# Two graph layers on one Trainium2 core: layer 1's aggregation made of three single-pass products instead of one fp32 product

## What is computed

```python
# layer 0: four bilinear scores, one picked by the code in adj (0 or 1 here)
e_k = leaky((h * a_k) @ h.T)                      # slope 0.2
alpha = sigmoid(where(adj == k + 1, e_k, -inf))
x = layernorm(x + alpha @ h + bias)
# layer 1
H = x @ W;  s = H @ a_src;  d = H @ a_dst
e = where(adj != 0, exp(-leaky(s[:, None] + d[None, :])), 0)
x = layernorm(x + elu((e @ H) / e.sum(-1)))
```

## Time and profile before

| | us |
|---|---|
| median of three runs | 1340.65 (1339.58 to 1341.52) |
| the profiled execution | 1340.03 |
| its span, first to last instruction | 1338.2 |
| one graph in the middle | 80.80 |
| TensorE busy | 1278.7 (96%) |
| VectorE, ScalarE, GpSimd busy | 1011.8, 855.6, 780.4 |
| TensorE's granted clock | 0.995 of full |

### The profile page before, as it was taken

How to read it: one execution, slowest core, us unless ns; L and a number is a source line. 1 busy time by engine, 2 the same in 40 slices (tenths; PEclk the granted TensorE clock), 3 DMA queues, 4 the chain that set the end, 5 groups by cost and what they waited for, 6 DMA issues and landing times.

```text
span 1338.2 us, 27323 instructions
## 1 busy us (share of the span) xinstructions
PE 1278.7 (96%) x7874; PEld 1142.2 (85%) x7874; DVE 1011.8 (76%) x2594; ACT 855.6 (64%) x2130; POOL 780.4 (58%) x1116
## 2 busy tenths in 40 slices
PE   5899999999999999999999999999999999999986
PEld 4888889898898988889888898988989888898875
DVE  4677778778787877778777787877878777787864
ACT  4756757576575766757577575766757567575643
POOL 3746648375573855638465583755738465483732
PEclk9999999999999999999999999999999999999999
DMA  9383480925629174380925719165380834709001
GB/s 208 64 157 92 97 145 12 186 65 118 125 39 171 49 141 110 77 159 15 173 78 106 137 27 177 55 133 114 56 183 16 161 90 98 141 18 189 25 5 34
DMA packets 223632, 135.29 MB, mean 101 GB/s; under 512 B 141168, under 2 KB 207088, under 8 KB 223600
## 3 DMA queue, kind: packets, MB, share of 16 engines
q1 hardware_dynamic: 188528, 84.57, 27.0%
q0 software_dynamic: 35072, 50.34, 23.4%
HBM read 101.32 MB, written 16.78 MB: 88 GB/s over the span
## 4 chain that ended last, share of the span: by engine, by line
PE 39%; POOL 24%; DVE 19%; issue 10%; ACT 6%; DMA 0%; DVEq 0%; POOLq 0%; ACTq 0%
POOL coef_lo L380 14%; PE acc_bank L1232 10%; PE hh_bank L1211 7%; DVE coef L885 5%; PE lg_bank L1113 4%; PE acc_bank L1115 3%; PE acc_bank L1113 3%; PE acc_bank L1114 3%; PE lg_bank L1115 3%; PE lg_bank L1114 3%; POOL rstd L401 3%; POOL rstd L391 2%; POOL var_eps L388 2%; DVE stats L925 2%; DVE reluP L920 2%
## 5 line engine op out<-in xcount | busy, mean ns | idle before, releaser
L1232 PE MATMUL acc_bank<-H,coef 128*128 128x258 f32 x2048 | 468.9, 382 | 10.9 <-ACT reluP L611 9.6
L1232 PEld LDWEIGHTS acc_bank<-H,coef 128*128 128x128 f32 x2048 | 381.6, 190 | 73.6 <-issue 20.2
L380 POOL TENSOR_TENSOR coef_lo<-coef,coef_hi 128x1024 fp32r<-128x1024 f32 x128 | 304.4, 2379 | 93.1 <-ACT coef_hi L557 93.1
L1113 PE MATMUL acc_bank<-h_hi,coef_hi 128*128 128x256 f32 x1024 | 302.7, 296 | 0.0
L1115 PE MATMUL acc_bank<-h_hi,coef_lo 128*128 128x256 f32 x1024 | 285.0, 278 | 0.0
L1114 PE MATMUL acc_bank<-h_lo,coef_hi 128*128 128x256 f32 x1024 | 284.9, 278 | 0.0
L885 DVE SCALAR_TENSOR_TENSOR coef<-tr_bank,E_col,codeT 128x256 f32<-128x256 f32 x512 | 209.2, 476 | 40.1 <-PE acc_bank L1232 36.8
L1113 PEld LDWEIGHTS acc_bank<-h_hi,coef_hi 128*128 128x128 f32 x1024 | 193.2, 189 | 3.2
L1114 PEld LDWEIGHTS acc_bank<-h_lo,coef_hi 128*128 128x128 f32 x1024 | 193.8, 189 | 1.8
L1115 PEld LDWEIGHTS acc_bank<-h_hi,coef_lo 128*128 128x128 f32 x1024 | 193.2, 189 | 0.0
L557 ACT ACTIVATE coef_hi<-coef 128x1024 fp32r<-128x1024 f32 x128 | 136.1, 1063 | 71.9 <-DVE coef L824 71.2
(11 more groups left out here) (77 smaller groups left out, 2192.3 us busy)
## 6 DMA issues: line engine op xcount, KB each, us to landing
code_nat<-in_adj POOLq DMA_DIRECT2D x128, 256.0 KB, 5.7
x_raw<-in_x SPq DMA_DIRECT2D x16, 1024.0 KB, 5.6
xb<-bias_bc SPq DMA_DIRECT2D x16, 1024.0 KB, 9.1
xb<-in_x POOLq DMA_DIRECT2D x16, 1024.0 KB, 12.3
out<-x SPq DMA_DIRECT2D x128, 128.0 KB, 1.7
codeT<-code_nat SPq DMA_TRANSPOSE x128, 3.8
W_ext<-in_L_gnn_W SPq DMA_DIRECT2D x1, 256.0 KB, 4.0
eluE<-in_L_gnn_a SPq DMA_DIRECT2D x1, 256.0 KB, 5.3
```

The lines of the kernel that those rows point to most:

```text
L380: nc.gpsimd.tensor_tensor(coef_lo[:, t % 4, :, :], blocks(coef[:, t % 4, :]), f32(coef_hi[:, t % 4, :, :]), ALU.subtract).then_inc(S.lo0, 1)
L1113: nc.tensor.matmul(dst, lhs_hi, rhs_hi, start=first, stop=False)
L1232: ins = nc.tensor.matmul(acc_bank[t % 2][:, 0:HC], coef[:, SLOT1[t], J * P:(J + 1) * P], H[:, J, :], start=J == 0, stop=J == NT - 1)
```

## The change

What it does, part by part:

- H is kept as `H_hi` and `H_lo` (fp32r), and aggregation 1 becomes three single-pass products a block on `coef_hi` and `coef_lo`, as in layer 0. The two extra `coef` buffers go; both layers share four (`t % 4`).
- ScalarE gets `high1` for each tile of layer 1, GpSimd `low1`. Tile 0 is split in two parts: blocks 0 to 4 ahead (`high1_begin`, `low1_begin`), 5 to 7 later.
- H of tiles 0 to 4 is staged in `xb` and split in one go (`high_H_first` on ScalarE, `low_H_first` on GpSimd). H of tiles 5 to 7 is written to `H_hi` directly, and VectorE makes `H_lo` (`low_H`). Projections 6 and 7 and the next graph's first wait for that.
- The masks of tiles 0 to 3 are made by instructions of four tiles (512 columns), those of 4, 5 and 6, 7 by pairs.
- `reluP` and its statistics have four buffers for two; the exponential goes to the free half of `xt_bank` in PSUM, one buffer, for two in SBUF. `power1` and the norms take two tiles at a time and come later.
- Chunk 2 moves on TensorE from behind transposes 6 to step 7, ahead of projection 5.
- SyncE also waits for `H_first_lo` before it fills `xb`; `add_x` and the low parts of x move later on GpSimd.

```diff
             def aggregate1(S, b, t):
-                pe.wait_ge(S.mask1, NT * b + t + 1)
+                pe.wait_ge(S.lo1, NT * b + t + 1)
...
                 for J in range(NT):
-                    ins = nc.tensor.matmul(acc_bank[t % 2][:, 0:HC], coef[:, SLOT1[t], J * P:(J + 1) * P],
-                                           H[:, J, :], start=J == 0, stop=J == NT - 1)
+                    ins = split_products(acc_bank[t % 2][:, 0:HC], coef_hi[:, t % 4, J, :], coef_lo[:, t % 4, J, :],
+                                         H_hi[:, J, :], H_lo[:, J, :], J == 0, J == NT - 1)
...
+            def low1(S, b, t, j0=0):
+                pool.wait_ge(S.hi1, NT * b + t + 1)
+                nc.gpsimd.tensor_tensor(coef_lo[:, t % 4, j0:NT, :], blocks(coef[:, t % 4, j0 * P:N]),
+                                        f32(coef_hi[:, t % 4, j0:NT, :]), ALU.subtract).then_inc(S.lo1, 1)
+            def low_H_first(b):
+                pool.wait_ge(F.H_first, b + 1)
+                nc.gpsimd.tensor_tensor(H_lo[:, 0:FIRST, 0:D], xb[:, 0:FIRST, :], f32(H_hi[:, 0:FIRST, 0:D]),
+                                        ALU.subtract).then_inc(F.H_first_lo, 1)
...
+                low1_begin(b)
                 if nxt:
                     low_x(F, b + 1, 0)
-                    add_x(b + 1)
...
+                low1(F, b, 0, EDGE)
+                for t in range(1, 4):
+                    low1(F, b, t)
+                for t in range(4, NT):
+                    low1(F, b, t)
+                    if nxt and t < 7:
+                        low_x(F, b + 1, t - 3)
+                    if nxt and t == 5:
+                        add_x(b + 1)
+                    if t == 5:
+                        power1(F, b, 0, 2)
+                power1(F, b, 2, 2)
+                if nxt:
+                    low0(F, b + 1, 0)
+                    low0(F, b + 1, 1)
+                power1(F, b, 4, 2)
+                if nxt:
+                    low0(F, b + 1, 2)
+                    low0(F, b + 1, 3)
...
+            def low_H(S, b, t):
+                dve.wait_ge(S.H, NT * b + t + 1)
+                nc.vector.scalar_tensor_tensor(H_lo[:, t, 0:D], hh_bank[:, 0:D], scale_col[:, t:t + 1],
+                                               f32(H_hi[:, t, 0:D]), ALU.mult, ALU.subtract).then_inc(S.H_lo, 1)
...
+                low_H(F, b, 5)
                 if nxt:
                     leaky_scores(b + 1, 3)
+                low_H(F, b, 6)
                 if nxt:
                     leaky_scores(b + 1, 4)
-                mask1_pair(b, 0, prev, EDGE, NT)
+                mask1_tiles(b, 0, 4, EDGE, NT)
+                low_H(F, b, 7)
+                ends_H_lo(F, b)
                 watch_sd(F, b, prev)
                 if nxt:
                     leaky_scores(b + 1, 5)
-                mask1_pair(b, 2, prev, EDGE, NT)
-                if nxt:
                     leaky_scores(b + 1, 6)
                 keep_watch(b, prev)
...
+                if nxt:
+                    leaky_scores(b + 1, 7)
+                mask1_tiles(b, 4, 2)
+                row_inverse(F, b, 0, prev)
+                if nxt:
+                    leaky_scores(b + 1, 8)
+                for t in range(NT):
+                    if t >= 3:
+                        row_inverse(F, b, t, prev)
+                    if t >= 4 and nxt:
+                        mask0_below(b + 1, t - 4, True)
+                        mask0_rest(b + 1, t - 4)
+                    residual1(F, b, t, prev)
+                    stats1(F, b, t)
+                    moments1(F, b, t)
                     if t < 2:
-                        mask1_pair(b, 2 * t + 4, prev)
+                        row_inverse(F, b, t + 1, prev)
+                    if t == 0:
+                        if nxt:
+                            leaky_row(b + 1, 3)
+                        mask1_tiles(b, 6, 2)
                     if nxt and t == 1:
-                        leaky_row(b + 1, 3)
...
+                        leaky_row(b + 1, 4)
```

More of the change, by code:

```diff
@@ L81, in __init__ @@
         self.H = sem(tag + "H")
+        self.H_lo = sem(tag + "H_lo")
+        if not general:
+            self.H_first = sem(tag + "H_first")
+            self.H_first_lo = sem(tag + "H_first_lo")
         self.ones = sem(tag + "ones")
-        self.squares = sem(tag + "squares")
+        self.ones_lo = sem(tag + "ones_lo")
         self.range_seen = sem(tag + "range_seen")
@@ L192, in two_graph_layers @@
         watch_max = sb("watch_max", [P, NT])
-        coef = sb("coef", [P, 6, N])
+        coef = sb("coef", [P, 4, N])
         coef_hi = sb("coef_hi", [P, 4, NT, P], FP32R)
@@ L296, in graph @@
                 if nxt:
-                    sp.wait_ge(F.resid0, NT * b + NT)
-                    sp.sem_inc(sp_past, 1)
+                    for made, count in ((F.resid0, NT * b + NT), (F.H_first_lo, b + 1)):
+                        sp.wait_ge(made, count)
+                        sp.sem_inc(past, 1)
                     fill_bias()
@@ L590, in keep_H, with high_H_first @@
                 act.wait_ge(S.scale, NT * b + t + 1)
-                nc.scalar.activation(H[:, t, 0:D], hh_bank[:, 0:D], ACT.Copy,
+                nc.scalar.activation(xb[:, t, :] if S is F and t < FIRST else H_hi[:, t, 0:D], hh_bank[:, 0:D], ACT.Copy,
                                      scale=scale_col[:, t:t + 1]).then_inc(S.H, 1)
+            def high_H_first(b):
+                act.wait_ge(F.H, NT * b + FIRST)
+                nc.scalar.activation(H_hi[:, 0:FIRST, 0:D], xb[:, 0:FIRST, :], ACT.Copy).then_inc(F.H_first, 1)
             def ends_H(S, b):
-                nc.scalar.activation(H[:, :, D], scale_col[:, :], ACT.Copy).then_inc(S.ones, 1)
+                nc.scalar.activation(H_hi[:, :, D], scale_col[:, :], ACT.Copy).then_inc(S.ones, 1)
             def last_G(b):
@@ L616, in norm1 @@
                 act.wait_ge(S.shift1, NT * b + t + 1)
-                nc.scalar.activation(x1[:, t, :], reluP[:, t % 2, :], ACT.Identity, bias=shift[:, t % 2, :],
-                                     scale=rstd[:, 2 + t % 2, :]).then_inc(S.y, 1)
+                nc.scalar.activation(x1[:, t, :], reluP[:, t % 4, :], ACT.Identity, bias=shift[:, t % 4, :],
+                                     scale=rstd[:, 2 + t % 4, :]).then_inc(S.y, 1)
             def graph(b, prev, nxt):
                 for t in range(NT + 1):
+                    if nxt and t == 8:
+                        scale_scores(b + 1, 2)
                     if t >= 3:
@@ L633, in graph @@
                     if t == 5 and prev:
+                        norm1(F, b - 1, NT - 2)
                         norm1(F, b - 1, NT - 1)
-                    if nxt and 6 <= t:
+                    if nxt and 6 <= t < 8:
                         scale_scores(b + 1, t - 6)
@@ L736, in _ @@
                         act.wait_ge(GEN.leaky1, NT * b + t + 1)
-                        nc.scalar.activation(coef[:, SLOT1[t], :], coef[:, SLOT1[t], :], ACT.Exp,
+                        nc.scalar.activation(coef[:, t % 4, :], coef[:, t % 4, :], ACT.Exp,
                                              scale=-1.0).then_inc(GEN.exp1, 1)
+                        high1(GEN, b, t)
                         elu_parts(GEN, b, t)
@@ L750, in _ @@
             dve.wait_ge(setup_step, 3)
-            nc.vector.tensor_copy(H[:, :, D + 1], sd_sq[:, :, 0]).then_inc(setup_step, 1)
+            for part in (H_hi, H_lo):
+                nc.vector.tensor_copy(part[:, :, D + 1], sd_sq[:, :, 0]).then_inc(setup_step, 1)
             def extend_weights(which, col):
                 for dt in range(KD):
-                    steps = 4 + 4 * (1 - which) + 2 * dt
+                    steps = 5 + 4 * (1 - which) + 2 * dt
                     dve.wait_ge(setup_step, steps)
```

297 lines of the change are left out of this document (168 added, 129 removed).

## The result

| | before | after |
|---|---|---|
| median, us | 1340.68 (1339.58 to 1341.52) | 1410.38 (1407.98 to 1410.77) |
| profiled span | 1338.2 | 1408.7 |
| one graph in the middle | 80.80 | 85.50 |
| mean granted TensorE clock | 0.995 | 0.973 |

The ratio is 1.0517 (95% interval 1.0498 to 1.0535): 70 us slower, where 16 us faster was forecast, and outside the range. The rows of after are read against those of before.

What follows compares the result with a forecast made beforehand. TensorE bounds the kernel, VectorE nearly as late. VectorE's 651.5 + 34.55 work + 8.7 waits gave 694.75, 1.0 us less a graph; with 1.5 in the last graph, 1340.03 - 16.5 = 1323.5, forecast 1324, range 1284 to 1352.

Steps and rivals of the forecast that it cites:

- part (b) of the waits: VectorE instructions with two SBUF inputs wait until GpSimd's instruction is over: 5.6 us a graph.
- TensorE's gain: Aggregation 1 tiles fall from 3.49 to 2.83 us: 0.66 us a tile, 84 us in 16 graphs.
- The head: Start of aggregation 1: ScalarE's new split and VectorE's difference of H 5 delay projections 6 and 7, 0.8 us lost.
- VectorE's chain: VectorE from E of tile 7 to residual 0 of the next graph: 34.55 us work plus 8.7 us waits.
- The waits for relu 0 to 3: VectorE waits for ScalarE, whose relus come after splits and scaling, before the residuals: 3.1 us a graph.
- The masks: Layer 0 masks of tiles 0 to 3 held by GpSimd differences: 1.3 us for the first, 1.8 for the others.
- The watch operations: Small VectorE operations and H's end column in aggregation 1, held by GpSimd differences: 1.2 and 1.3 us.
- My own test for rival 1: In the new trace, watch operations keeping 0.16 us and TensorE 99% busy would show TensorE stays the bound.
- rival 1: TensorE stays the bound, VectorE's waits under 4.45 us a graph: 1256, or 1284 with waits of 6 us; chance 0.23.
- rival 2: Slower: GpSimd's layer 1 differences stop VectorE, deciding from 9.7 us of waits; 1367, or 1350 at 10.4 us; chance 0.27.
- the seven meetings: Four masks, end column, range pair and code watch meeting GpSimd differences, on average 1.2 us each, 8.4 us.
- Rival 3: Three products not faster where weights are loaded three times: at or above 1340; no chance of its own, counted with slower.

Runs made afterwards that it cites:

- the best version: The 1320 us version with chunk 5 made leaky on VectorE ahead of the difference of H 7: 1309.68 us, ratio 0.9771.
- run 73: Not a run label: the words say that the whole run saves 73 to 81 us, for 84 forecast.
- the norm free: Changed kernel with one wait more: GpSimd's difference of H's tiles 0 to 4 starts only after norm 7 of layer 0: 1355.59 us, ratio 1.0119.
- the 1320 us version: Changed kernel with GpSimd held until norm 7 is done, and its differences beside the layer 0 masks held until masks are made: 1319.98 us, ratio 0.9848.
- the reordered version: The 1320 us version with chunk 5 before H 7's difference, chunk 6 before the watch operations, ScalarE's split of H 0 to 4 after x1T 6: 1354.8 us.

## Why the prediction was wrong

**The step that failed** is the rule in part (b) of the waits: "an instruction with two inputs in SBUF waits until GpSimd's is over". It was drawn from masks and a PSUM mask and then read backwards: what has not two SBUF tiles as inputs is free. The norm has one, and two scalar columns beside it, so it was in no list, neither of meetings nor of rivals. Yet the text let ScalarE's split of H, which GpSimd's difference of 2.9 us follows, end at 645.5, and in the kernel before the norm of tile 7 starts inside those 2.9 us:

```profile
646.30 0.40 DVE L854 TENSOR_SCALAR x<-resid,moments,rstd 128x256 f32<-128x256 f32 x1
```

It is held all the same (2.48 us for 0.41), 54.8 us of the 69.7. Whether it is held because of its scalar columns or because of the way a VectorE instruction from SBUF to SBUF runs, no run here separates. Reading one SBUF tile is not enough by itself: the statistics of a residual read one, and took their 0.43 us beside a GpSimd difference that had begun just before, and no more than 0.43 in any of their 128 times:

```profile
784.09 0.43 DVE L1022 BATCH_NORM_STATS2 stats<-reluP 128x6 f32<-128x256 f32 x1
784.08 2.41 POOL L402 TENSOR_TENSOR coef_lo<-coef,coef_hi 128x1024 fp32r<-128x1024 f32 x1 [0.80 <-ACT coef_hi L612]
```

The Trainium skill (SBUF — State Buffer, Who interferes with whom) names `tensor_scalar`, `copy` and `cast` in their two-port modes as contending too; the trace agrees that this `tensor_scalar` is held, but shows nothing of a faster mode: alone it takes 0.41 us, as long as the residual of the same size with an input in PSUM. The prediction had cited only the half of that section on two inputs. The kernel before held a hint as well: its 128 norms all take 0.40 to 0.42 us in a kernel whose GpSimd is 58% busy, and there `low0` waits for `x1` of a tile before it starts, though `hi0`, which it waits for too, already implies that its buffer is free. A wait that no data needs may be such a guard; no run here takes it out.

**The clock** was in no term. The wait of 3 us a graph on TensorE cost the run 21.9 us more than its length.

**TensorE's gain** was sized a little too large. Behind mirrors a tile of aggregation 1 takes 2.95 us (796.93 to 799.88) for 2.83 forecast, elsewhere 2.85 to 2.89. Start to start, with the same six transposes between, tile 5 takes 4.15 us before and 3.52 after:

```profile
677.62 3.65 PE L1232 MATMUL acc_bank<-H,coef 128*128 128x258 f32 x16
681.77 3.65 PE L1232 MATMUL acc_bank<-H,coef 128*128 128x258 f32 x16
```

```profile
796.93 0.36 PE L1220 MATMUL acc_bank<-H_hi,coef_hi 128*128 128x258 f32 x1
800.45 0.37 PE L1220 MATMUL acc_bank<-H_hi,coef_hi 128*128 128x258 f32 x1
```

Tile 0 with chunk 8 behind it takes 4.53 and 3.96. So a tile saves 0.57 to 0.63 us for 0.66, and the run 73 to 81 us for 84. Of these the best version kept 31.

**The head** was forecast to lose 0.8 us. Measured from the start of aggregation 0 of tile 2, projection 6 came at 35.41 us in the changed kernel (766.49 - 731.08) and at 33.24 with the norm free (735.98 - 702.74), for 31.41 before: 4.0 and 1.8. So even without the norm the term was 1 us a graph short.

**VectorE's chain**, the number the forecast stood on, was close where the norm is free: from E of tile 7 to residual 0 it takes 43.88 us (740.00 to 783.88) for 43.25. But its parts were not all right. The waits for relu 0 to 3 are 2.9 us (0.49, 0.28, 1.18, 0.98) for 3.1. The masks lose 4.1 us (2.19, 0.98, 1.19 and 1.66 us for the four tiles, less the 0.28, 0.42, 0.55 and 0.68 that they take alone in the 1320 us version) for 3.1. The watch operations lose nothing in the changed kernel, 0.16 us each as before, for 2.5; waits of 1.40 ahead of chunk 7 and of 0.63 for the `coef` buffer of tile 1 came in their place. My own test for rival 1, watch operations at 0.16 us, came out true, and the rival with it did not: it also wanted TensorE full. The rule behind them was right, as the 2.3 us each in the reordered version show; only GpSimd had a gap at that moment.

With these the forecast of 79.83 us a graph becomes 79.83 + 1.08 for the later E + 0.63 for the chain + 0.17 up to the aggregation = 81.71, the graph with the norm free. The other 3.8 us of the 85.5 are the norm and its clock, and 15 times that is 57 us, against the 54.8 that the hold gave.

**The rivals.** The direction was rival 2's, differences on GpSimd that stop VectorE, and its masks are part of it (holding GpSimd until they are over gained 35.6 us, some of it in meetings that the kernel before had too). But it had priced the seven meetings and at most 1367; the eighth was the dear one. Rival 3 (three products no faster) is excluded.

**Still open**: why the best version stops at 1310, 42 to 50 us above what TensorE's own gain would allow; the waits left on TensorE are mostly of 1.2 us and less, and were not taken apart further. One place to look: its 96 masks of 512 columns still take 1.27 us in the mean (1.20 in the kernel before), where one alone takes 0.68. How much of that is on the path was not tried. Nor was the move of chunk 2 undone alone.

## What to carry to other kernels

Before work goes to GpSimd, list every VectorE instruction that can stand beside it with two SBUF inputs, or with one tile and scalar columns, those of eight columns too: a held one takes what is left of the GpSimd instruction, whatever its own size. Then ask which of them a wait hangs on, and hold GpSimd until that one is over; here five such waits turned 1410 us into 1320 with no work removed. A stall is worth removing only if what stands behind it on its engine does not wait for the same thing.

## What was not expected of the hardware

- A norm of 128x256 (one SBUF tile, two scalar columns) takes 0.41 us alone and 2.48 us when a GpSimd difference of 128x1280 started 0.39 us before it; instructions of 8 and 16 columns take 0.16 us and 2.02 to 2.32 us. VectorE instructions with an operand in PSUM kept their 0.42 us, and the statistics, with one SBUF tile and no scalar columns, their 0.43: the residual groups were never stretched.
- The granted clock fell to 0.93 of full over the 24 us behind a TensorE wait of 3.03 us, and not when dummy transposes filled that wait; it was worth 21.9 us in the run. Waits of 0.96 and 1.25 us left it at 1.00.
- One more GpSimd instruction of some 2.3 us a graph (its busy time rises from 780.4 to 816.8 us over 16 graphs) cost the old kernel 15 us, and nothing when it began behind the norm.
